# Query rows prepared 128 at a time and transposed by DMA instead of TensorE, in a fused cross attention and quantised FFN

## What is computed

```python
q = (layernorm(x) @ Wq).reshape(b, 256, 16, 128) / sqrt(128)
k, v = (ctx @ Wk), (ctx @ Wv)              # same shape
attn = softmax(einsum('bqhd,bkhd->bhqk', q, k))
x1 = x + einsum('bhqk,bkhd->bqhd', attn, v).reshape(b, 256, 2048) @ Wo
out = x1 + ffn(layernorm(x1))
```

## Time and profile before

| | before |
|---|---|
| median of 3 runs | 2190.7 us (2190.6 to 2194.46) |
| the profiled execution | 2190.88 us, span 2189.3 us |
| mean granted TensorE clock | 0.986 |
| TensorE busy | 2085.6 us, 95% |
| VectorE, ScalarE, GpSimd busy | 1533.2, 1035.8, 791.9 us |
| share of the ending chain on TensorE | 80% |
| DMA | 179.55 MB, mean 82 GB/s |

### The profile page before, as it was taken

One profiled execution on the slowest core, in us unless ns is written; L12 is line 12 of the kernel. 1 busy time (PEld: TensorE's weight loads), 2 busy tenths in 40 slices (PEclk: granted clock), 3 DMA queues, 4 the chain that ended last, 5 costly groups with the idle time before them and its releaser, 6 DMA issues.

```text
span 2189.3 us, 49860 instructions
## 1 busy us (share of the span) xinstructions
PE 2085.6 (95%) x15818; PEld 1535.8 (70%) x15818; DVE 1533.2 (70%) x3455; ACT 1035.8 (47%) x2760; POOL 791.9 (36%) x1093
## 2 busy tenths in 40 slices
PE   6899999999999999999999999999999978999996
PEld 5678777877787877777787877787888853444442
DVE  6777776777777776777676767676665548777774
ACT  7755554555555554545454545455544532333331
POOL 4333333332333333333232323331111006666664
PEclk9999999999999999999999999999999998999998
DMA  6733433232333333333333333232232253544444
GB/s 219 185 79 73 83 69 88 64 78 69 79 73 78 74 76 76 76 76 76 72 76 76 76 76 76 67 74 62 61 63 59 52 152 65 85 82 84 84 84 66
DMA packets 398607, 179.55 MB, mean 82 GB/s; under 512 B 361984, under 2 KB 374784, under 8 KB 398400
## 3 DMA queue, kind: packets, MB, share of 16 engines
q1 hardware_dynamic: 375616, 125.10, 27.7%
q0 software_dynamic: 16608, 45.36, 8.5%
q10 hardware_dynamic: 6176, 6.29, 0.9%
HBM read 61.08 MB, written 27.26 MB: 40 GB/s over the span
## 4 chain that ended last, share of the span: by engine, by line
PE 80%; issue 4%; DVE 4%; DMA 4%; POOL 3%; ACT 3%; SPq 1%; POOLq 0%; DVEq 0%; ACTq 0%
PE b_qk L1019 30%; PE b_v L1019 15%; PE b_o L1074 7%; PE b_c L1019 7%; PE b_s L1019 7%; PE b_w L1074 7%; DMA attn_weights<-x_scratch 2%; POOL attn_weights L514 2%; PE b_pt L1019 1%; DMA probT<-psplit 1%; PE b_x L1019 1%; PE b_w L1162 1%; PE b_x L1026 1%; DVE inner_amax L951 1%; SPq L328 1%
## 5 line engine op out<-in xcount | busy, mean ns | idle before, releaser
L559 ACT ACTIVATE qk<-b_qk 128x512 f16<-128x512 f32 x256 | 152.7, 596 | 663.6 <-PE b_s L1019 663.5
L857 DVE TENSOR_REDUCE nmax<-b_s 128x2 f32<-128x512 f32 x257 | 177.7, 691 | 371.9 <-PE b_s L1019 371.9
L1019 PE MATMUL b_qk<-xT,attn_weights 128*128 (+1 forms) x3072 | 382.8, 275 | 25.6 <-issue 23.8
L1019 PE MATMUL b_v<-attn_weights,kvT 128*128 128x256 f16 x3072 | 377.2, 273 | 8.0 <-POOL attn_weights L390 8.0
L1019 PE MATMUL b_qk<-kvT,attn_weights 128*128 (+1 forms) x3072 | 384.6, 276 | 0.0
L1019 PEld LDWEIGHTS b_qk<-xT,attn_weights 128*128 128x128 f16 x3072 | 301.6, 99 | 66.2 <-issue 26.9
L881 DVE SCALAR_TENSOR_TENSOR psplit<-prob,rrec,psplit 128x256 f16<-128x256 f32 x514 | 287.1, 600 | 80.5 <-ACT psplit L600 80.5
L1019 PEld LDWEIGHTS b_qk<-kvT,attn_weights 128*128 128x128 f16 x3072 | 304.4, 99 | 38.5
L1019 PEld LDWEIGHTS b_v<-attn_weights,kvT 128*128 (+1 forms) x3072 | 300.2, 98 | 43.8 <-issue 9.0
L600 ACT ACTIVATE psplit<-prob,rrec 128x256 f16<-128x256 f32 x514 | 233.0, 500 | 95.9 <-DVE rrec L874 95.6
L590 ACT ACTIVATE prob<-b_s,nmax 128x256 f32<-128x256 f32 x514 | 238.8, 469 | 33.3 <-DVE nmax L857 1.6
(11 more groups left out here) (124 smaller groups left out, 2736.7 us busy)
## 6 DMA issues: line engine op xcount, KB each, us to landing
ffn_w<-wffn SPq DMA_DIRECT2D x48, 256.0 KB, 3.2
acc<-xtok POOLq DMA_DIRECT2D x16, 512.0 KB, 4.0
out<-acc POOLq DMA_DIRECT2D x16, 512.0 KB, 4.3
out<-attn_weights POOLq DMA_DIRECT2D x32, 256.0 KB, 4.1
xrow<-xq POOLq DMA_DIRECT2D x61, 128.0 KB, 3.7
kvrow<-kvt POOLq DMA_DIRECT2D x61, 128.0 KB, 3.3
stage<-wattn SPq DMA_DIRECT2D x12, 512.0 KB, 3.8
ffn_scratch<-ffn_t SPq DMA_DIRECT2D x48, 128.0 KB, 1.8
```

Of the source, the lines that this page charges most:

```text
L559: eng.activation(dst, src, ACT.Copy, scale=scale).then_inc(sm[done], 1)
L857: eng.tensor_reduce(nmax[:, :], bS[:, :].rearrange("p (q f) -> p q f", q=2), AX_X, ALU.max, negate=True).then_inc(sm["max_done"], 1)
L1019: last = eng.matmul(out, l, r, start=(a == 0), stop=(a == len(pairs) - 1))
```

## The change

x is prepared 128 rows (one tile m) in two quads, 2m and 2m + 1. VectorE's statistics (k = 0) and normalisation (k = 3) and ScalarE's hi part (end of k = 3) are in the even quad; VectorE's lo part is at k = 0 of the odd quad. Hi and lo are made from the rows as they are, into the new tile xsplit (128x1024 float16), and SP transposes xsplit into xT by one DMA, behind the probability transpose of k = 1 of the odd quad. TensorE's x_transpose is gone; before the first quad of a batch it waits for the tiles to have landed. GpSimd does rstd in even quads; in odd quads it waits for the normalised rows and loads the next tile, now 128x512 from the tensor xtok. The loops of SP and ScalarE now have two quads as their body; their and VectorE's first quads are written out. The input xq is dropped. The core of the diff:

```diff
@@ tensors
-        xrow = sb("xrow", D, F32, ROWS)
-        xnorm = sb("xnorm", D, F32, ROWS)
+        xrow = sb("xrow", D, F32)
+        xnorm = sb("xnorm", D, F32)
+        xsplit = sb("xsplit", 2 * D, F16)
...
+        def x_part(part):
+            return xsplit[:, :].rearrange("p (c h f) -> p h c f", c=KC, h=2)[:, part]
@@ SP
+            def transpose_x(m):
+                wait_apart(eng, "x_lo", m + 1)
+                eng.dma_start_transpose(xT[:, bass.ds(((m + 2) & 3) * 1024, 1024)].rearrange("p (j f) -> p j f", j=8),
+                                        xsplit[:, :]).then_inc(sm["xT_loaded"], 16)
...
-            def ffn_quad(n, store=True, load=True):
+            def ffn_quad(n, store=True, load=True, m=None):
                 for k in range(QUAD):
                     transpose_p(4 * n + k, k % 2)
+                    if m is not None and k == 1:
+                        transpose_x(m)
                     if store and k == 0:
                         store_ffn(n - FFN_FROM - 1)
...
+                    if n % 2 and k == 1:
+                        transpose_x(n // 2)
                     for g in (EARLY + PIECES * n + 2 * k, EARLY + PIECES * n + 2 * k + 1):
@@ GpSimd
-            def load_x(r):
-                eng.dma_start(xrow[:, :], xq[bass.ds((r + QPB) & (NQ - 1), 1), :, :].rearrange("g p f -> p (g f)")
+            def load_x(m):
+                eng.dma_start(xrow[:, :], xtok.rearrange("b t p d -> (b t) p d")[bass.ds((m + 2) & (TILES - 1), 1), :, :]
...
-            def prep(r):
-                rstd(ROWS, 1, "aggr_done", "rstd_step", "rstd_done", r)
-                wait_apart(eng, "xn_ready", r + 1)
-                load_x(r + 1)
+            def prep(r, m, odd):
+                if odd:
+                    wait_apart(eng, "xn_ready", m + 1)
+                    load_x(m + 1)
+                else:
+                    rstd(P, 1, "aggr_done", "rstd_step", "rstd_done", m)
@@ ScalarE
             def x_prep(m):
-                hi(prep_slot(xT, m + QPB, 0), bX[:, 0:KC * ROWS].rearrange("p (c f) -> p c f", c=KC), X_SCALE,
-                   "x_tr", m + 1, "x_hi")
+                if not isinstance(m, int) or m > 0:
+                    eng.wait_ge(sm["xT_loaded"], 16 * m)
+                hi(x_part(0), xnorm[:, :].rearrange("p (c f) -> p c f", c=KC), X_SCALE, "xn_ready", m + 1, "x_hi")
...
-                    if prepare and k == 2:
-                        x_prep(n)
+                    if m is not None and k == 3:
+                        x_prep(m)
@@ VectorE
             def x_apply(m):
-                eng.wait_ge(sm["x_tr"], m)
                 eng.wait_ge(sm["rstd_done"], m + 1)
-                apply(xnorm[:, :], xrow[:, :], ROWS).then_inc(sm["xn_ready"], 1)
+                apply(xnorm[:, :], xrow[:, :], P).then_inc(sm["xn_ready"], 1)
             def x_lo(m):
-                lo(prep_slot(xT, m + QPB, 1), bX[:, 0:KC * ROWS].rearrange("p (c f) -> p c f", c=KC),
-                   prep_slot(xT, m + QPB, 0), X_SCALE, "x_hi", m + 1, "x_lo")
+                lo(x_part(1), xnorm[:, :].rearrange("p (c f) -> p c f", c=KC), x_part(0), X_SCALE, "x_hi", m + 1, "x_lo")
...
+                m, odd = 2 * s + q // 2, q % 2
...
-                    if prepare and k == 0:
-                        x_stats(n)
+                    if prepare and k == 0 and odd:
+                        x_lo(m)
+                    if prepare and k == 0 and not odd:
+                        x_stats(m)
...
-                    if prepare and k == 3:
-                        x_lo(n)
+                    if prepare and k == 3 and not odd:
+                        x_apply(m)
...
-                    if prepare and k == 1:
-                        x_apply(n)
@@ TensorE
-            def x_transpose(m):
-                eng.wait_ge(sm["xn_ready"], m + 1)
-                wait_apart(eng, "x_lo", m)
-                for c in range(KC):
-                    last = eng.transpose(bX[:, c * ROWS:(c + 1) * ROWS], xnorm[:, c * P:(c + 1) * P],
-                                         ident[0:ROWS, 0:ROWS])
-                last.then_inc(sm["x_tr"], 1)
...
-                    if prepare and k == 2:
-                        x_transpose(n)
...
-            def ready(n):
-                eng.wait_ge(sm["x_lo"], n)
+            def ready(n, first):
+                if first:
+                    eng.wait_ge(sm["xT_loaded"], 8 * n)
                 eng.wait_ge(sm["kv_lo"], n)
```

More of the change, by code:

```diff
@@ L74, with build @@
 PARTS = ((0, 0), (0, 1), (1, 0))
-def build(nc, xq, kvt, wattn, wffn, xtok, out):
+def build(nc, kvt, wattn, wffn, xtok, out):
     xqs = nc.dram_tensor("x_scratch", (TILES, P, D), BF16, kind="Internal").ap()
@@ L178, in build @@
             stage_loaded0 stage_loaded1 stage_loaded2 stage_loaded3 piece_hi piece_lo_even piece_lo_odd
-            x_loaded kv_loaded stats_done aggr_done rstd_step rstd_done xn_ready x_tr x_hi x_lo kv_hi kv_lo
+            x_loaded kv_loaded stats_done aggr_done rstd_step rstd_done xn_ready x_hi x_lo xT_loaded kv_hi kv_lo
             s_done max_done exp_done sum_scaled rec_done
@@ L294, in ffn_quad, with odd @@
                         load_ffn(w + 1)
+            def odd(n):
+                return (n - 1) // 2 if n % 2 and n < NQ - 4 else None
             for n in range(QPB):
@@ L303, in _ @@
             ffn_quad(FFN_FROM, store=False)
[L304 to L309, removed]
+            ffn_quad(FFN_FROM + 1, m=odd(FFN_FROM + 1))
+            with eng.Fori(FFN_FROM // 2 + 1, FFN_TO // 2 - 1) as m:
+                ffn_quad(2 * m)
+                ffn_quad(2 * m + 1, m=m)
+            for n in range(FFN_TO - 2, FFN_TO + 2):
+                ffn_quad(n, store=(n <= FFN_TO), load=(n < FFN_TO - 1), m=odd(n))
+            with eng.Fori(FFN_TO // 2 + 1, NQ // 2 - 2) as m:
+                ffn_quad(2 * m, store=False, load=False)
+                ffn_quad(2 * m + 1, store=False, load=False, m=m)
             for n in range(NQ - 4, NQ):
@@ L361, in _ @@
                 eng.memset(z[:, :].bitcast(F32), 0.0).then_inc(sm["zeroed"], 1)
-            def load_x(r):
-                eng.dma_start(xrow[:, :], xq[bass.ds((r + QPB) & (NQ - 1), 1), :, :].rearrange("g p f -> p (g f)")
-                              ).then_inc(sm["x_loaded"], 16)
+            def load_x(m):
+                eng.dma_start(xrow[:, :], xtok.rearrange("b t p d -> (b t) p d")[bass.ds((m + 2) & (TILES - 1), 1), :, :]
+                              .rearrange("g p f -> p (g f)")).then_inc(sm["x_loaded"], 16)
             def load_kv(r):
@@ L460, in batch @@
                     if prepare:
-                        prep(n)
+                        prep(n, 2 * s + q // 2, q % 2)
                     if ffn:
@@ L579, in kv_prep, with quad @@
                    "kv_loaded", 16 * (m + 1), "kv_hi")
-            def quad(n, front=True, split=0, ffn=False, prepare=True):
+            def quad(n, front=True, split=0, ffn=False, prepare=True, m=None):
                 for k in range(QUAD):
@@ L647, in _, with even @@
                 split_piece(0, pc)
[L648 to L652, removed]
-            quad(FFN_FROM + 1, ffn=True)
[L654 to L657, removed]
+            def even(n):
+                return None if n % 2 else n // 2
+            for n in range(QPB):
+                quad(n, split=QUAD // 2 if n == QPB - 1 else QUAD, m=even(n))
+            quad(FFN_FROM, m=even(FFN_FROM))
+            quad(FFN_FROM + 1, ffn=True)
+            with eng.Fori(FFN_FROM // 2 + 1, FFN_TO // 2) as m:
+                quad(2 * m, ffn=True, m=m)
+                quad(2 * m + 1, ffn=True)
+            quad(FFN_TO, ffn=True, m=even(FFN_TO))
+            quad(FFN_TO + 1)
+            with eng.Fori(FFN_TO // 2 + 1, NQ // 2 - 2) as m:
+                quad(2 * m, m=m)
+                quad(2 * m + 1)
             for n in range(NQ - 4, NQ - 1):
@@ L714, in x_stats @@
                 eng.wait_ge(sm["x_loaded"], 16 * (m + 1))
-                eng.bn_stats(stat[0:ROWS, 0:6], xrow[:, :]).then_inc(sm["stats_done"], 1)
+                eng.bn_stats(stat[:, 0:6], xrow[:, :]).then_inc(sm["stats_done"], 1)
                 wait_apart(eng, "stats_done", m + 1)
-                eng.bn_aggr(mv[0:ROWS, 0:2], stat[0:ROWS, 0:6]).then_inc(sm["aggr_done"], 1)
+                eng.bn_aggr(mv[:, 0:2], stat[:, 0:6]).then_inc(sm["aggr_done"], 1)
             def apply(dst, src, rows, tile_=0):
@@ L934, in _ @@
                 split_piece(0, pc)
[L935 to L938, removed]
+            for n in range(QPB):
+                quad(n, split=QUAD // 2 if n == QPB - 1 else QUAD, s=0, q=n)
             quad(FFN_FROM, ffn=True, s=0, q=QPB)
@@ L1076, in project, with quad, quad_at @@
                 last.then_inc(sm["o_done"], 1)
-            def quad(n, fresh=False, ffn=False, prepare=True):
+            def quad(n, fresh=False, ffn=False):
                 q = n % QPB if isinstance(n, int) else None
-                quad_at(n, (n + QPB - 1) // QPB - 1, q, fresh, ffn, prepare)
```

(19 more changed lines are left out.)

## The result

| | before | after |
|---|---|---|
| median | 2191.86 us (4 runs) | 2163.29 us (4 runs, 2160.9 to 2165.1) |
| the profiled execution | 2190.88, span 2189.3 | 2160.9, span 2159.3 |

The ratio is 0.9868, with a 95% interval of 0.985 to 0.9885: 28.6 us less by the medians, 30.0 by the profiled executions. The forecast was 2155.5 us.

The account below looks back on a forecast made before the run. TensorE, 98% busy from 134 to 1700 us, was taken to bound the long stage, with other engines co-deciding in the first four quads. 2190.9 - 27.4 (transposes) - 8.0 (first four quads) = 2155.5 us, range 2146 to 2172.

Parts of the forecast that it names:

- The transposes that go: TensorE, quads 0 to 59: four fp32 transposes cost 0.49 us per quad; 56 quads behind the first four give 27.4 us.
- The page figure: TensorE transposes: the skill's 275 ns each would give 1.1 us per quad, 61.6 us for 56 quads.
- VectorE and ScalarE, nothing: Long stage: both engines get lighter, but neither sets the pace while TensorE is 98% busy, so no time is won.
- The DMA transposes, nothing: SP queue, odd quads: 30 new x transposes, 1.24 us to issue each, taken as 0 between bounds 0 and 37 us.
- rival (d): Odd quads: x transposes block the probability transposes, so the kernel gets slower, 2198 us at a 5.05 us landing; chance 0.04.
- What is late next: Context product of k=3 waiting for the probabilities of k=2: time in hand falls from 1.1 to 0.6 us, still enough.
- Rival (b): At k=3, 0.6 us in hand isn't enough as landings stretch; 0.49 us given back in 48 quads, 2179 us; chance 0.10.
- The first four quads: 20 to 134 us: GpSimd's split waits go, some DMA waits and transposes too; 8 us taken, between 2 and 12.8.
- my upper bound: First four quads: 12.8 us at most, from 8.0 of GpSimd waits, 2.8 of DMA waits and 2.0 of transposes.
- Rival (a): First four quads give only their 2.0 us of transposes, as ScalarE and DMA landings pace them: 2161.5 us; chance 0.18.
- The gaps: Ten TensorE gaps ending in "issue" at its loop body's end, 23.8 us, and the lower clock behind some: no change taken.
- the sum of the prediction: Whole kernel: 27.4 us for the transposes and 8.0 us for the first four quads, 35.4 us less.

Follow-up runs that it names:

- the order alone: Kernel before, with GpSimd in the first four quads no longer waiting for normalised rows and loading the next ones ahead of its weight splits: 2184.38 us, ratio 0.9967.
- pad84: Changed kernel with 84 semaphore increments behind TensorE's first two waits, bringing its loop back to its old instruction count: 2166.5 us.
- the four kernels of the table: The kernel before, the changed kernel, pad46, and a padded changed kernel with idle transposes back only in the last quad ahead of each loop edge (2206.79 us).
- pad46: Changed kernel with 46 semaphore increments behind TensorE's first two waits, meant to put the loop's start just behind a 16 KB block's end: 2197.14 us.
- pad64: Changed kernel with 64 semaphore increments behind TensorE's first two waits, meant to put the block's end just ahead of the loop's start: 2163.33 us.

## Why the prediction was right, and where it was off

The range (2146 to 2172) and the side held; the middle was 7.8 us too low.

- **The transposes that go, 27.4 us:** right. Head period 7.03 to 6.53 us, no wait in its place; put back they cost 27.5 us. The page figure that would have made 61.6 us of it (the Trainium skill, TensorE: Matmul & The Clock Gate, Part 4: PE-mode transpose), stated for another shape and type, does not carry over to these.
- **VectorE and ScalarE, nothing:** right. The sizes taken were 0.53, 0.69 and 0.6 us, measured 0.599, 0.751 and 0.621.
- **The DMA transposes, nothing:** right, landing 3.1 us in the median, and 1.9 us at most when left out. With it rival (d) falls (its 5.05 us would have been 1.45 us per odd quad and not 1.43, 2199 in place of 2198). The page's preference for TensorE (the Trainium skill, VectorE: DVE Perf Modes, Rules for kernel authors) does not hold here, where TensorE is what bounds.
- **What is late next, 0.6 us in hand:** held, with not one DMA wait from quad 4 to 1680; at 912.55 TensorE's context product comes 0.56 us after its probabilities landed. Rival (b) falls. But the smaller margin had a price at the loop edge, which I had not seen (below).
- **The first four quads, 8 us of 12.8:** 7.4 us measured, 7.1 with the order alone. The GpSimd waits of the v projection went, but 3.2 us of shorter ones on the same splits came. The 2.0 us of transposes that my upper bound held do not show, and other profiles of the same early program give 5.1 to 7.9 us, so that 8 and 7.4 lie so close is in part luck. Rival (a) falls.
- **The gaps, "I take no change":** this step failed. I took "the loop body stays" for "its edges stay". The change takes 84 instructions out ahead of the loop, which moves the loop's start against the 16 KB blocks: 7 second gaps of some 1 us, +6.5 us. And the branch stays tied to the landing of a probability transpose, so that the 0.49 us of the head ahead of an edge turn into idle time: first gaps of 2.83 in place of 2.38 us, +4.5 us. The second point also bears on the first term: of the 27.4 us some 5 were given back at the ten edges. The profiled run got 4.7 back by fewer stretches at the lower clock, which is chance as far as these runs show (pad84 has six again). Without this the forecast would have been off by more. The remaining 2.4 us between it and the median can be one or two such stretches, of 1.6 us each: the three other runs have a mean granted clock of 0.987 to 0.988, the profiled one 0.99; no profile of them is at hand.

Taken without loops the sum of the prediction, 35.4 us, was measured as 35.2 by the medians. The profiled spans give 32.5, with 5.1 of the 8.0 us that were forecast ahead of quad 4, so the match of the first figure is closer than that of its parts.

## What to carry over

Where one engine is busy for 98% of a stage, the head period from the chain, with and without the operation, prices its removal; the busy time per instruction doesn't. But work that is removed just ahead of a wait and a loop branch can come back as idle time behind it. Where gaps end in "issue" behind a loop's branch, count them before anything else: here, with the lower clock behind them, they cost 40 us, more than the change won, and with the number of instructions ahead of the loop alone their sum went from 28 to 53 us. Write such a loop out, or try a few offsets, before judging a small change; then look for the edges of the other engines' loops, which come to light only then.

## What I had not expected of the hardware

- A branch back leaves TensorE idle for 2.0 to 3.2 us while a block of instructions comes, and for 5.3 us in the mean where the 16 KB block ends 4 matmuls behind the target. The matmuls resume 3.7 to 4.5 us behind the start of the branch, and the next block lands 5.5 to 6.5 us behind it, in all the kernels above in which the loop stands. 46 idle instructions, hidden behind TensorE's first wait, made the kernel 34 us slower (2163.29 to 2197.14).
- The branch itself waits its turn behind the last semaphore wait of the loop's body: 0.15 us after the landing at the edges of the four kernels of the table. What TensorE still has to do at that moment, 1.23 or 1.73 us, is what hides part of the fetch.
- In pad46 an idle time of 5.3 us in two pieces is followed by the lower clock at all ten edges; in before, after, pad64 and pad84 the first gaps of 2.1 to 3.2 us are at three to seven of ten.
- A semaphore increment on TensorE's queue takes 0.15 us ((30.2 - 16.8) / 88, as above).
